# Cross-attention on one core: moving the tiles that TensorE reads to other addresses in SBUF

## The chip, the core and the metric

The kernel runs on one core of a Trainium2 chip. The metric is the device time of one execution in microseconds, as the median of several runs. The engines are TensorE (PE, with its weight loads as PEld), VectorE (DVE), ScalarE (ACT), GpSimd (POOL) and SyncE (SP, which only issues transfers here).

## What is computed

Eight sequences, each with 256 query rows of width 256 and 256 context rows of width 192; 16 heads of 64:

```
h    = layernorm(x) * gamma + beta
Q, K, V = h @ Wq, context @ Wk, context @ Wv      # 16 heads of 64
attn = softmax(Q K^T, axis=-1) * 64 ** -0.5
out  = x + (attn @ V).reshape(...) @ Wo + bo
```

## The kernel before

All weights stay in SBUF, each as a high part (`w_hi`, type float32r) and the rest (`w_lo`); the products of float32r tiles are made in three passes (high by high, high by low, low by high). One step `u` does two of the eight head pairs of a sequence, so four heads, and there are 32 steps, four for each sequence. PE's program in one step, in this order (lines of the profile in brackets):

- `values_rest` (L893): the last pass of V for this step, in two halves of 64 rows, with `c_rest` and `c_t` stationary;
- `scores` (L700): Q stationary, K moving, 12 pairs of 64-row matmuls of 256 columns, the two of a pair side by side in the two halves of the array; Q and K are slots 1 and 0 of `qk_hi` and `qk_lo`;
- `keys_rest` (L771): one pair of 64-row matmuls, `w_lo` stationary;
- `mix` (L729): 16 float32 matmuls, `v_sb` stationary (64 columns), `prob_t` moving;
- `keys` and `queries` (L753, L793): for each of two head pairs 4 and 6 matmuls of 256 columns, weights stationary, the context `c_t` or `h_hi`/`h_lo` moving: 20 in all;
- `output` (L818): 12 matmuls, `mix_hi`/`mix_lo` stationary, weights moving;
- `turn` (L846): 16 float32 transposes of 128 columns, of `prob` against the unit matrix `ident`; once per sequence 4 more each for the context (L675) and x (L683);
- `values` (L880): 8 matmuls, `c_t` stationary, weights moving.

In words of the hardware's program each matmul is a weight load (the stationary operand) and a matmul that streams the moving operand; PE loads the next matmul's weights while the present one streams.

The other engines work beside this. ACT makes the exponentials (L407), the high parts of Q and K (L417), of the mix (L435), V's copy (L395) and half of the copies of the turned probabilities (L460). DVE makes the row maxima (L565), reciprocals, the low parts (L578, L613) and the other copies (L644). POOL scales the probabilities (L319). PE waits at fixed places on them: `scores` on Q's and K's low parts and on the copies of the turned probabilities, `keys_rest` on V's copy, `output` on the mix's low part, `turn` on POOL's scaled probabilities, one wait for each of four heads.

**Homes.** The tensors lie in SBUF in the order in which they are declared, each on the same bytes of every partition; each size is rounded up to a multiple of 32 bytes, and `w_raw`, the first, begins at a multiple of 128 bytes. Worked out from the declared shapes, the homes modulo 128 before the change are:

| tiles | bytes modulo 128 before | after |
|---|---|---|
| `w_raw`, `w_hi`, `w_lo`, `ident`, `v_sb` | 0 | 0 |
| `h_hi`, `h_lo`, `c_t`, `c_rest` | 0 | 64 |
| Q in `qk_hi`, `qk_lo` | 0 | 0 |
| K in `qk_hi`, `qk_lo` | 0 | 64 |
| `x_norm` | 0 | 64 |
| `c_in`, `prob`, `prob_t`, `mix_hi`, `mix_lo` | 96 | 64 |
| `x_in`, `y_sb` | 96 | 0 |

All slices that PE takes of these tiles begin at a multiple of 512 bytes from the tile's (or Q's or K's) beginning, so the table holds for every operand.

Of the kernel before, what the change touches and what calls it, by code (L numbers as in the profile page):

```python
# [5 lines left out]
def cross_attention_block(nc, x, ctx_in, w_q, w_k, w_v, w_o, b_o, gamma, beta, out):  # L6
# [4 lines left out]
    fp32 = mybir.dt.float32  # L11
# [48 lines left out]
    LO_VECTOR = (0, 4, 5, 8, 9, 13, 16)  # L60
    LO_POOL = (1, 2, 3, 6, 7, 10, 11, 12, 14, 15, 17, 18, 19, 20, 21, 22, 23)
    WARM = 6
    V_HALF = GROUP * P // 2

    with ExitStack() as ctx:
# [6 lines left out]
        def sem(name):  # L72
            return ctx.enter_context(nc.semaphore(name))

        w_raw = sb("w_raw", [P, TILES, INNER])
        w_hi = sb("w_hi", [P, TILES, INNER], fp32r)
        w_lo = sb("w_lo", [P, TILES, INNER], fp32r)
        ident = sb("ident", [P, P])
        gamma_c = sb("gamma_c", [P, DT])
        beta_c = sb("beta_c", [P, DT])  # L80
        bo_b = sb("bo_b", [P, D])
        neg_half = sb("neg_half", [P, RT])
        x_in = sb("x_in", [P, 2, RT, D])
        c_in = sb("c_in", [P, 2, RT, D_CTX])
        bn = sb("bn", [P, RT, 6])
        mean_var = sb("mean_var", [P, RT, 2])
        var_eps = sb("var_eps", [P, RT])
        rstd = sb("rstd", [P, RT])
        x_norm = sb("x_norm", [P, RT, D])
        x_bias = sb("x_bias", [P, 2, RT, D])  # L90
        h_full = sb("h_full", [P, DT, ROWS])
        h_hi = sb("h_hi", [P, 2, DT, ROWS], fp32r)
        h_lo = sb("h_lo", [P, 2, DT, ROWS], fp32r)
        c_t = sb("c_t", [P, 2, CT, ROWS], fp32r)
        c_rest = sb("c_rest", [HALF, 2, ROWS], fp32r)
        qk_hi = sb("qk_hi", [P, BATCH, 2, ROWS], fp32r)
        qk_lo = sb("qk_lo", [P, BATCH, 2, ROWS], fp32r)
        v_sb = sb("v_sb", [P, 2, RT, GROUP * P])
        neg_max = sb("neg_max", [P, HEADS, RT])
        sums = sb("sums", [P, HEADS, RT])  # L100
        inv = sb("inv", [P, HEADS, RT])
        prob = sb("prob", [P, HEADS, RT, ROWS])
        prob_t = sb("prob_t", [P, HEADS, RT, ROWS])
        mix_hi = sb("mix_hi", [P, BATCH, ROWS], fp32r)
        mix_lo = sb("mix_lo", [P, BATCH, ROWS], fp32r)
        y_sb = sb("y_sb", [P, 2, RT, D])

        st_ps = [bank(f"st{e}_ps") for e in range(HEADS)]
        mix_ps = bank("mix_ps")
# [237 lines left out]
        def _(act):  # L347
# [38 lines left out]
            def step(u, turns):  # L386
                def values_out(n, ps):
                    act.wait_ge(v_made, n + 1)
                    nc.scalar.activation(v_sb[:, n // RT % 2, n % RT, :], ps[:, :], ACT.Copy)\
                        .then_inc(v_ready, 1)  # L390

                if 2 <= u < STEPS:
                    act.wait_ge(v_made, u + 1 + turns(8))
                    for k, ps in enumerate((w0_ps, w1_ps)):
                        last = nc.scalar.activation(  # L395
                            v_sb[:, u // RT % 2, u % RT, k * V_HALF:(k + 1) * V_HALF],
                            ps[:, 0:V_HALF], ACT.Copy)
                    last.then_inc(v_ready, 1)
                if u == 1:
                    act.wait_ge(c_turned, 2)  # L400
                    context_hi(1, context_bank(1))

                def probabilities(e):
                    if 0 <= u < STEPS:
                        act.wait_ge(max_ready, HEADS * u + e + 1 + turns(32))
                        for r in range(RT):
                            last = nc.scalar.activation(prob[:, e, r, :],  # L407
                                                        st_ps[e][:, r * ROWS:(r + 1) * ROWS],
                                                        ACT.Exp, bias=neg_max[:, e, r:r + 1],
                                                        accum_out=sums[:, e, r:r + 1])  # L410
                        last.then_inc(prob_ready, 1)

                def keys_hi(a):
                    t = BATCH * u + BATCH + a
                    if t < BATCH * STEPS:
                        act.wait_ge(projected, t + 1 + turns(16))
                        nc.scalar.activation(qk_hi[:, a, :, :].rearrange("p a b -> p (a b)"),  # L417
                                             qk_banks(u)[a][:, :], ACT.Copy)\
                            .then_inc(qk_hi_ready, 1)

                if u == 1:
                    weight_hi(14)
                probabilities(0)
                probabilities(1)
                if u in (1, 2):
                    weight_hi({1: 15, 2: 21}[u])
                if u == STEPS:

                    for a in range(BATCH):
                        act.wait_ge(mixed, u + a)  # L430
                        nc.scalar.activation(mix_hi[:, a, :], (mix_ps, w0_ps)[a][:, 0:ROWS],
                                             ACT.Copy).then_inc(mix_hi_ready, 1)
                elif 1 <= u < STEPS:
                    act.wait_ge(mixed, u + turns(8))
                    nc.scalar.activation(mix_hi[:, :, :].rearrange("p a b -> p (a b)"),  # L435
                                         mix_ps[:, :], ACT.Copy).then_inc(mix_hi_ready, 1)
                probabilities(2)
                keys_hi(0)
                if u == -1:
                    weight_hi(6)  # L440
                    weight_hi(7)
                probabilities(3)
                keys_hi(1)
                if u == -1:
                    weight_hi(8)
                    weight_hi(9)
                if u == 0:
                    values_out(0, w0_ps)
                    weight_hi(10)
                    weight_hi(11)  # L450
                    values_out(1, w1_ps)
                if u == 1:
                    weight_hi(16)
                if 0 <= u < STEPS:
                    if u >= 1:

                        act.wait_ge(mixed, u + turns(8))
                    for e in range(0, HEADS, 2):
                        act.wait_ge(turned, HEADS * u + e + 1 + turns(32))
                        nc.scalar.activation(prob_t[:, e, :, :].rearrange("p a b -> p (a b)"),  # L460
                                             st_ps[e][:, :], ACT.Copy)\
                            .then_inc(prob_t_ready[0], 1)
                        if u == 0 and e == 0:
                            weight_hi(12)
                            weight_hi(13)
                b = of_seq(u, TURN_C, 2)
                if b is not None:
                    act.wait_ge(c_turned, b + 1 + turns(2))
                    context_hi(b, context_bank(b))
                b = of_seq(u, TURN_X, 1)  # L470
                if b is not None:

                    act.wait_ge(h_lo_ready, DT * b + turns(4))
                    act.wait_ge(x_turned, b + 1 + turns(2))
                    hidden(b, mix_ps)
                for n in {1: (17, 18, 19, 20), 2: (22, 23)}.get(u, ()):
                    weight_hi(n)
# [7 lines left out]
        def _(dve):  # L485
# [59 lines left out]
            def step(u, turns):  # L545
# [28 lines left out]
                def keys_lo(a):  # L574
                    t = BATCH * u + BATCH + a
                    if t < BATCH * STEPS:
                        dve.wait_ge(qk_hi_ready, t + 1 + turns(16))
                        nc.vector.tensor_tensor(qk_lo[:, a, :, :].rearrange("p a b -> p (a b)"),  # L578
                                                qk_banks(u)[a][:, :],
                                                qk_hi[:, a, :, :].rearrange("p a b -> p (a b)")  # L580
                                                .bitcast(fp32), ALU.subtract)\
                            .then_inc(qk_lo_ready, 1)

                maximum(0)
# [76 lines left out]
        def _(pe):  # L661
# [26 lines left out]
            def scores(u):  # L688
                for a in range(BATCH):
# [6 lines left out]
                    for r in range(RT):  # L696
                        for n, (q, key) in enumerate(passes):
                            for h in range(2):
                                own = slice(h * HALF, (h + 1) * HALF)
                                last = nc.tensor.matmul(  # L700
                                    st_ps[2 * a + h][:, r * ROWS:(r + 1) * ROWS],
                                    q[own, a, 1, r * P:(r + 1) * P], key[own, a, 0, :],
                                    start=n == 0, stop=n == len(passes) - 1)
                                if r == RT - 1 and n == len(passes) - 1:
                                    last.then_inc(scores_made, 1)
# [273 lines left out]
```

## Time and profile before

| | |
|---|---|
| median of 3 runs | 359.43 us (359.4 to 359.51) |
| the profiled execution's own time | 359.32 us |
| its span, first to last instruction | 357.5 us |
| busy: PE, PEld, ACT, DVE, POOL | 97%, 87%, 72%, 68%, 46% |
| TensorE's granted clock | 1.0 throughout (2.4 GHz) |

The profiled execution is 0.11 us under the median, and 1.8 us of it lie outside the span. Matmuls overlap in their records: one takes some 270 to 290 ns from its start to its end, while the next begins 109 to 120 ns after it. So the spacing of the starts tells the rate, and the duration tells a stall of the stream on top of a fixed latency.

### The profile page before, as it was taken

The numbers are of one execution on the slowest core, as the hardware profiler recorded it, in microseconds if no ns is written. First come the engines' busy times: TensorE is split into PE (matmuls) and PEld (weight loads), VectorE is DVE, ScalarE is ACT, GpSimd is POOL, SyncE is SP. The second block draws the span as 40 slices with busy tenths as digits, with TensorE's granted clock in tenths as the row PEclk, the third lists the DMA queues.
The fourth block names the chain that finished last, engine by engine and source line by source line (L and its number), as shares of the span: only waits on it lengthen the run. The fifth ranks groups of instructions, "written<-read, shape, count | busy, mean of one in ns | idle before, by whom it ended". The sixth has DMA issues, their size and how long they took to land.

```text
span 357.5 us, 9031 instructions
## 1 busy us (share of the span) xinstructions
PE 347.6 (97%) x3266; PEld 309.9 (87%) x3266; DVE 244.0 (68%) x534; ACT 256.6 (72%) x800; POOL 164.6 (46%) x321
## 2 busy tenths in 40 slices
PE   5999999999999999999999999999999999999986
PEld 5779888889888889988889988889988889988875
DVE  5897657865768667676677676776576856566654
ACT  4898877776778766878667776777677876677762
POOL 4576894226443263443632465322744325344331
PEclk9999999999999999999999999999999999999999
DMA  6940010020001100020000200002000000000000
GB/s 186 273 131 3 1 53 2 3 81 2 3 0 44 42 2 0 2 81 2 3 2 0 83 2 0 2 2 81 2 2 0 31 2 2 0 4 30 2 2 29
DMA packets 10756, 10.61 MB, mean 30 GB/s; under 512 B 960, under 2 KB 10176, under 8 KB 10720
## 3 DMA queue, kind: packets, MB, share of 16 engines
q1 hardware_dynamic: 10192, 9.64, 8.8%
q8 instruction: 26, 0.43, 0.5%
q10 hardware_dynamic: 416, 0.33, 0.3%
q0 software_dynamic: 112, 0.13, 0.2%
q14 instruction: 10, 0.08, 0.1%
HBM read 8.00 MB, written 2.10 MB: 28 GB/s over the span
## 4 chain that ended last, share of the span: by engine, by line
PE 92%; ACT 3%; DVE 2%; POOL 1%; issue 1%; DVEq 0%; POOLq 0%; ACTq 0%
PE mix_ps L729 16%; PE st_ps L846 15%; PE o_ps L818 12%; PE w_ps L793 12%; PE st_ps L700 12%; PE w_ps L753 10%; PE w_ps L880 8%; PE w_ps L893 3%; ACT prob L407 2%; PE w_ps L771 1%; PE mix_ps L683 1%; PE o_ps L670 1%; PE mix_ps L675 1%; ACT qk_hi L417 0%; DVE w_lo L492 0%
## 5 line engine op out<-in xcount | busy, mean ns | idle before, releaser
L319 POOL TENSOR_SCALAR prob<-prob,inv 128x256 f32<-128x256 f32 x256 | 120.3, 486 | 152.9 <-DVE inv L572 152.9
L407 ACT ACTIVATE prob<-st_ps,neg_max 128x256 f32<-128x256 f32 x256 | 118.4, 476 | 23.6 <-DVE neg_max L565 23.6
L565 DVE TENSOR_REDUCE neg_max<-st_ps 128x2 f32<-128x512 f32 x128 | 82.0, 683 | 27.0 <-PE st_ps L700 25.9
L460 ACT ACTIVATE prob_t<-st_ps 128x512 f32<-128x512 f32 x64 | 38.4, 600 | 40.2 <-PE st_ps L846 40.2
L644 DVE COPY prob_t<-st_ps 128x512 f32<-128x512 f32 x64 | 44.1, 691 | 28.5 <-PE st_ps L846 25.1
L729 PE MATMUL mix_ps<-prob_t,v_sb 128*64 128x256 f32 x504 | 61.4, 386 | 0.1
L846 PE MATMUL st_ps<-ident,prob 128*128 128x128 f32 x512 | 61.1, 273 | 0.0
L846 PEld LDWEIGHTS st_ps<-ident,prob 128*128 128x128 f32 x512 | 56.7, 141 | 0.1
L578 DVE TENSOR_TENSOR qk_lo<-w_ps,qk_hi 128x512 fp32r<-128x512 f32 x62 | 42.8, 690 | 17.7 <-ACT qk_hi L417 17.7
L407 ACT ACTIVATION_READ_ACCUMULATOR prob<-st_ps,neg_max 128x1 f32 x256 | 53.4, 209 | 0.0
L729 PEld LDWEIGHTS mix_ps<-prob_t,v_sb 128*64 128x64 f32 x504 | 33.4, 136 | 17.9 <-issue 0.3
L417 ACT ACTIVATE qk_hi<-w_ps 128x512 fp32r<-128x512 f32 x62 | 37.9, 612 | 1.2 <-PE w_ps L793 1.2
L700 PE MATMUL st_ps<-qk_hi 64*128 64x256 f32 x256 | 36.6, 282 | 0.9 <-DVE prob_t L644 0.6
L753 PEld LDWEIGHTS w_ps<-c_t,w_hi 128*128 128x128 f32 x186 | 26.3, 190 | 11.8 <-issue 11.2
L700 PE MATMUL st_ps<-qk_lo,qk_hi 64*128 64x256 f32 x256 | 36.2, 279 | 0.0
L818 PE MATMUL o_ps<-w_hi,mix_hi 128*128 128x256 f32 x124 | 34.8, 281 | 1.4 <-DVE mix_lo L613 1.4
L700 PE MATMUL st_ps<-qk_hi,qk_lo 64*128 64x256 f32 x256 | 36.1, 279 | 0.0
L753 PE MATMUL w_ps<-c_t,w_hi 128*128 128x256 f32 x186 | 35.5, 300 | 0.0
L818 PE MATMUL o_ps<-w_hi,mix_lo 128*128 128x256 f32 x124 | 34.8, 280 | 0.0
L818 PE MATMUL o_ps<-w_lo,mix_hi 128*128 128x256 f32 x124 | 34.7, 280 | 0.0
L395 ACT ACTIVATE v_sb<-w_ps 128x256 f32<-128x256 f32 x60 | 19.7, 381 | 19.6 <-PE w_ps L893 18.9
L880 PE MATMUL w_ps<-w_hi,c_t 128*128 128x256 f32 x180 | 32.3, 296 | 0.0
(137 smaller groups left out, 646.9 us busy)
## 6 DMA issues: line engine op xcount, KB each, us to landing
x_in<-in_x_dram SPq DMA_DIRECT2D x8, 256.0 KB, 3.2
out_dram<-y_sb SPq DMA_DIRECT2D x7, 256.0 KB, 2.2
c_in<-in_ctx_dram SPq DMA_DIRECT2D x7, 192.0 KB, 3.1
w_raw<-in_L_xattn_Wq_dram SPq DMA_DIRECT2D x8, 128.0 KB, 3.1
w_raw<-in_L_xattn_Wo_dram SPq DMA_DIRECT2D x4, 256.0 KB, 4.4
w_raw<-in_L_xattn_Wk_dram SPq DMA_DIRECT2D x4, 128.0 KB, 4.1
w_raw<-in_L_xattn_Wk_dram SPq DMA_DIRECT2D x8, 64.0 KB, 3.5
w_raw<-in_L_xattn_Wv_dram SPq DMA_DIRECT2D x2, 256.0 KB, 4.7
```

Of the source, the lines that this page charges most:

```text
L319: last = nc.gpsimd.tensor_scalar(prob[:, e, r, :], prob[:, e, r, :], inv[:, e, r:r + 1], SCALE, ALU.mult, ALU.mult)
L407: last = nc.scalar.activation(prob[:, e, r, :], st_ps[e][:, r * ROWS:(r + 1) * ROWS], ACT.Exp, bias=neg_max[:, e, r:r + 1], accum_out=sums ...
L565: nc.vector.tensor_reduce(neg_max[:, e, :], st_ps[e][:, :].rearrange("p (r j) -> p r j", r=RT), AX, ALU.max, negate=True).then_inc(max_rea ...
L578: nc.vector.tensor_tensor(qk_lo[:, a, :, :].rearrange("p a b -> p (a b)"), qk_banks(u)[a][:, :], qk_hi[:, a, :, :].rearrange("p a b -> p ( ...
L644: nc.vector.tensor_copy(prob_t[:, e, :, :].rearrange("p a b -> p (a b)"), st_ps[e][:, :]).then_inc(prob_t_ready[1], 1)
L700: last = nc.tensor.matmul(st_ps[2 * a + h][:, r * ROWS:(r + 1) * ROWS], q[own, a, 1, r * P:(r + 1) * P], key[own, a, 0, :], start=n == 0, ...
L729: last = nc.tensor.matmul(ps[h * HALF:(h + 1) * HALF, first:first + ROWS], v_sb[:, w // RT % 2, j, p * P + h * HALF:p * P + (h + 1) * HALF ...
L753: nc.tensor.matmul(ps[:, 0:ROWS], w[:, i, cols], c_t[:, b % 2, k, :], start=not shared and w is w_hi and i == K0 and k == 0, stop=w is pas ...
L793: last = nc.tensor.matmul(ps[:, ROWS:2 * ROWS], w[:, Q0 + d, cols], h[:, b % 2, d, :], start=n == 0 and d == 0, stop=n == 2 and d == DT - ...
L818: last = nc.tensor.matmul(o_ps[:, r * D:(r + 1) * D], m[:, a, r * P:(r + 1) * P], wt[:, O0 + o, cols], start=s == 0 and a == 0 and n == 0 ...
L846: last = nc.tensor.transpose(st_ps[e][:, j * ROWS + r * P:j * ROWS + (r + 1) * P], prob[:, e, r, j * P:(j + 1) * P], ident[:, :])
L880: nc.tensor.matmul((w0_ps, w1_ps)[a][:, 0:V_HALF], c_t[:, b % 2, k, rows], w[:, i, first:first + V_HALF], start=m == 0, stop=False, skip_g ...
```

## The change

The order of the declarations changes, two unused tiles of 64 bytes (`shift0`, `shift1`) are put in, and the tiles for Q and K get 16 unused elements (64 bytes) behind each slot, which puts K at 64 and Q at 0 modulo 128. The two instructions that write these tiles now write two runs of 256 elements in place of one run of 512, and `scores` takes the first 256 elements of K's slot. No instruction is added, removed or moved.

```
+    SHIFT = 16
...
         ident = sb("ident", [P, P])
+        sb("shift0", [P, SHIFT])
+        h_hi = sb("h_hi", [P, 2, DT, ROWS], fp32r)
+        h_lo = sb("h_lo", [P, 2, DT, ROWS], fp32r)
+        c_t = sb("c_t", [P, 2, CT, ROWS], fp32r)
+        c_rest = sb("c_rest", [HALF, 2, ROWS], fp32r)
+        mix_hi = sb("mix_hi", [P, BATCH, ROWS], fp32r)
+        mix_lo = sb("mix_lo", [P, BATCH, ROWS], fp32r)
+        qk_hi = sb("qk_hi", [P, BATCH, 2, ROWS + SHIFT], fp32r)
+        qk_lo = sb("qk_lo", [P, BATCH, 2, ROWS + SHIFT], fp32r)
+        c_in = sb("c_in", [P, 2, RT, D_CTX])
+        x_norm = sb("x_norm", [P, RT, D])
+        prob = sb("prob", [P, HEADS, RT, ROWS])
+        prob_t = sb("prob_t", [P, HEADS, RT, ROWS])
+        sb("shift1", [P, SHIFT])
+        v_sb = sb("v_sb", [P, 2, RT, GROUP * P])
...
-                        nc.scalar.activation(qk_hi[:, a, :, :].rearrange("p a b -> p (a b)"),
-                                             qk_banks(u)[a][:, :], ACT.Copy)\
+                        nc.scalar.activation(qk_hi[:, a, :, 0:ROWS],
+                                             qk_banks(u)[a][:, :].rearrange("p (a b) -> p a b", b=ROWS),
+                                             ACT.Copy)\
...
-                        nc.vector.tensor_tensor(qk_lo[:, a, :, :].rearrange("p a b -> p (a b)"),
-                                                qk_banks(u)[a][:, :],
-                                                qk_hi[:, a, :, :].rearrange("p a b -> p (a b)")
-                                                .bitcast(fp32), ALU.subtract)\
+                        nc.vector.tensor_tensor(qk_lo[:, a, :, 0:ROWS],
+                                                qk_banks(u)[a][:, :]
+                                                .rearrange("p (a b) -> p a b", b=ROWS),
+                                                qk_hi[:, a, :, 0:ROWS].bitcast(fp32),
+                                                ALU.subtract)\
...
-                                    q[own, a, 1, r * P:(r + 1) * P], key[own, a, 0, :],
+                                    q[own, a, 1, r * P:(r + 1) * P], key[own, a, 0, 0:ROWS],
```

## Rows read from the trace of the kernel before

**Rows 1.** The page: busy time, granted clock by slice, chain that ended last.

```profile
PE 347.6 (97%) x3266; PEld 309.9 (87%) x3266; DVE 244.0 (68%) x534; ACT 256.6 (72%) x800; POOL 164.6 (46%) x321
...
PEclk9999999999999999999999999999999999999999
...
PE 92%; ACT 3%; DVE 2%; POOL 1%; issue 1%; DVEq 0%; POOLq 0%; ACTq 0%
```

**Rows 2.** The waits: who waited for whom: us in total, times, longest.

```profile
PE o_ps L818 <- DVE mix_lo L613: 1.4, 1, 1.4
...
PE st_ps L700 <- DVE prob_t L644: 0.6, 1, 0.6
```

**Rows 3.** Timeline of PE in one step: start us, length us, group and its count.

```profile
151.49 0.28 PE L700 MATMUL st_ps<-qk_hi 64*128 64x256 f32 x2
...
152.93 0.28 PE L771 MATMUL w_ps<-c_rest,w_lo 64*128 64x256 f32 x1
...
155.59 0.40 PE L793 MATMUL w_ps<-h_hi,w_hi 128*128 128x256 f32 x2
...
157.51 0.28 PE L818 MATMUL o_ps<-w_hi,mix_hi 128*128 128x256 f32 x1
...
158.92 1.91 PE L846 MATMUL st_ps<-ident,prob 128*128 128x128 f32 x16
160.67 0.60 PE L683 MATMUL mix_ps<-ident,x_norm 128*128 128x128 f32 x4
...
161.58 0.52 PE L880 MATMUL w_ps<-w_hi,c_t 128*128 128x256 f32 x3
161.94 0.28 PE L880 MATMUL w_ps<-w_lo,c_t 128*128 128x256 f32 x1
```

**Rows 4.** Single lines, whole span: duration ns min/median/max, first and last start.

```profile
L793 PEld LDWEIGHTS w_ps<-h_hi,w_hi x124: 187/192/193, 9.6 to 337.4; 128*128 128x128 f32 x124
L793 PE MATMUL w_ps<-h_hi,w_hi x124: 281/283/301, 9.7 to 337.5; 128*128 128x256 f32 x124
...
L818 PEld LDWEIGHTS o_ps<-w_hi,mix_hi x124: 187/188/193, 28.8 to 348.4; 128*128 128x128 f32 x124
L818 PE MATMUL o_ps<-w_hi,mix_hi x124: 277/280/387, 29.0 to 348.5; 128*128 128x256 f32 x124
...
L700 PE MATMUL st_ps<-qk_lo,qk_hi x256: 274/280/285, 12.9 to 343.7; 64*128 64x256 f32 x128
...
L846 PE MATMUL st_ps<-ident,prob x512: 270/273/273, 19.7 to 350.5; 128*128 128x128 f32 x171
...
L893 PEld LDWEIGHTS w_ps<-w_lo,c_rest x30: 182/183/183, 33.6 to 342.3; 64*128 64x128 f32 x30
...
L867 PE MATMUL w_ps<-w_lo,c_t x4: 392/394/501, 18.0 to 19.5; 128*128 128x512 f32 x4
```

**Rows 5.** Timeline of the weight loads after a pause of the stream.

```profile
151.27 0.18 PEld L893 LDWEIGHTS w_ps<-w_lo,c_t 64*128 64x128 f32 x1
151.37 0.19 PEld L700 LDWEIGHTS st_ps<-qk_hi 64*128 64x128 f32 x2
```

**Rows 6.** Timelines of the same step: what PE waits for, and its loads.

```profile
151.69 0.66 ACT L395 ACTIVATE v_sb<-w_ps 128x256 f32<-128x256 f32 x2
...
152.81 0.19 PEld L771 LDWEIGHTS w_ps<-c_rest,w_lo 64*128 64x128 f32 x1
...
156.07 0.68 DVE L613 TENSOR_TENSOR mix_lo<-mix_ps,mix_hi 128x512 fp32r<-128x512 f32 x1
...
157.40 0.19 PEld L818 LDWEIGHTS o_ps<-w_hi,mix_hi 128*128 128x128 f32 x1
...
158.32 0.93 POOL L319 TENSOR_SCALAR prob<-prob,inv 128x256 f32<-128x256 f32 x2 [0.47 <-DVE inv L572]
```

**Rows 7.** Groups by line: DVE reading 512 elements as 2 x 256 and flat.

```profile
L565 DVE TENSOR_REDUCE neg_max<-st_ps 128x2 f32<-128x512 f32 x128 | 82.0, 683 | 27.0 <-PE st_ps L700 25.9
L644 DVE COPY prob_t<-st_ps 128x512 f32<-128x512 f32 x64 | 44.1, 691 | 28.5 <-PE st_ps L846 25.1
```

More of the change, by code:

```diff
@@ L78, in cross_attention_block @@
         ident = sb("ident", [P, P])
+        sb("shift0", [P, SHIFT])
[13 more added lines that the diff above has]
+        v_sb = sb("v_sb", [P, 2, RT, GROUP * P])
+        x_in = sb("x_in", [P, 2, RT, D])
+        x_bias = sb("x_bias", [P, 2, RT, D])
+        h_full = sb("h_full", [P, DT, ROWS])
+        y_sb = sb("y_sb", [P, 2, RT, D])
+        bo_b = sb("bo_b", [P, D])
         gamma_c = sb("gamma_c", [P, DT])
         beta_c = sb("beta_c", [P, DT])
-        bo_b = sb("bo_b", [P, D])
         neg_half = sb("neg_half", [P, RT])
-        x_in = sb("x_in", [P, 2, RT, D])
-        c_in = sb("c_in", [P, 2, RT, D_CTX])
         bn = sb("bn", [P, RT, 6])
@@ L88, in cross_attention_block @@
         rstd = sb("rstd", [P, RT])
[L89 to L98, printed above, removed]
         neg_max = sb("neg_max", [P, HEADS, RT])
@@ L101, in cross_attention_block @@
         inv = sb("inv", [P, HEADS, RT])
[L102 to L106, printed above, removed]
         st_ps = [bank(f"st{e}_ps") for e in range(HEADS)]
```

## The prediction

> **What bounds the kernel now.** I read the page first: PE is busy 97% of the span and carries 92% of the chain that ended last, at full clock in every slice [rows 1]. The reader should see that nothing but PE's own stream can give more than a few us. The table of waits came next: the largest waits of PE in the steady part are single ones, 1.4 and 0.6 us [rows 2], so PE isn't held up by others. What is left is the rate at which PE's instructions follow each other, so I read the timeline of one step for the spacing of starts, and then the durations by line.
>
> The spacing falls into three classes [rows 3]. Between 155.59 and 157.51 there are 16 matmuls of keys and queries: 1.92 / 16 = 120 ns each. Twelve score pairs from 151.49 to 152.93: 1.44 / 12 = 120 ns a pair. Values, 161.58 to 161.94: 0.36 / 3 = 120. The 12 of the output, 157.51 to 158.92: 1.41 / 12 = 117.5. The 16 transposes, 158.92 to 160.67: 1.75 / 16 = 109.4. Set beside the homes, the first class has both operands at 0 modulo 128 (distance 0), the output has 96 against 0 (32 bytes apart around the circle of 128), and the transposes are plain float32, not float32r, at 96 against 0 or (L683) 0 against 0.
>
> The durations say that the extra time is a stall and not a fixed cost [rows 4]. A transpose takes 273 ns, a query matmul 283, an output matmul 280: 10 and 7 ns more, near the 10.6 and 8.1 ns that the spacings differ by. The best score matmul takes 274, so a float32r stream of 256 columns can go without a stall. Weight loads show the same: 183 ns where no stream runs beside them (L893), 188 beside the output's, 192 beside the queries'. Stream and load slow each other, and by a little less at distance 32 than at distance 0.
>
> **The change, part by part.** Nothing is added or removed, so the sum is a count of spacings times a difference. After the change every pair of a load and a stream is 64 bytes apart modulo 128.
>
> Count. A step has 12 score pairs, 1 pair of L771, 20 keys and queries and 8 values at distance 0, that is 41, of which 2 or 3 begin a group after a change of kind and are spaced by that. I take 39 in 31 steps, 1200, and 12 x 31 = 372 of the output at distance 32.
>
> The price after the change isn't in the trace: no pair stands 64 bytes apart. Its bounds:
> - Best case: no stall, the transposes' 109.4, say 109. Saved 1200 x 11 + 372 x 8.5 ns = 13.2 + 3.2 = 16.4 us.
> - From distance 0 to 32 the spacing fell from 120 to 117.5. Twice as far on the same line gives 115: 1200 x 5 + 372 x 2.5 = 6.0 + 0.9 = 6.9 us.
> - No better than what 32 bytes gave (117.5): 1200 x 2.5 = 3.0 us.
> - Worst that the rows support: distance 64 is like 0 again; then the output goes back to 120, 372 x 2.5 = 0.9 us lost.
>
> I take the middle between the unstalled 109 and 117.5, rounded to 113, because 64 is the farthest that two homes can be from each other on a circle of 128, and because even within the stalled classes single matmuls reach 274 ns [rows 4]. 1200 x 7 + 372 x 4.5 = 8.4 + 1.7 = 10.1 us.
>
> The Trainium skill (TensorE: Matmul & The Clock Gate, Back-to-back issue gap) has a gap of N / 2.4 + 2.5 ns, which is 109 for 256 columns. [...] By that rule as the state after the change the sum would be the best case above, 343.0 us.
>
> Float32 work. The mix (L729) and the transposes change from distance 32 to 64, L683 from 0 to 64. The four transposes of x, at distance 0, last 0.60 us together, which less the last one's 273 ns is 0.327 / 3 = 109 ns a start [rows 3, 4], as those of the probabilities at distance 32. So the distance doesn't seem to matter to float32, and I cost it at nothing. If they began to stall like the others, 24 x 31 x 10 ns = 7.4 us would be lost.
>
> Evacuations. L417 and L578 now write two runs of 256. DVE already reads 512 elements as 2 x 256 in 683 ns and flat in 691 [rows 7], so I take nothing. Should each take 50 ns longer, it lies beside PE's output and transposes and is hidden: `qk` is wanted only in the next step.
>
> **Does the saving reach the end?** A step becomes at most 16.4 / 31 = 0.53 us shorter, and the waits' reserves must cover it [rows 6, 3]. V's copy ends 151.69 + 0.66 = 152.35, the load that waits for it starts at 152.81: reserve 0.46, against at most 12 x 11 = 0.13 saved between. The mix's low part ends 156.75, wanted at 157.40: 0.65, against 20 x 11 = 0.22. POOL ends the fourth head's scaling at 159.25; its transposes are the last four of the sixteen and begin 158.92 + 12 x 0.109 = 160.23: 0.98, against (33 x 11 + 12 x 8.5) = 0.47. All reserves stay, so what PE saves arrives at the end. The few single waits [rows 2] give back none of what is saved before them; I put 0.1 us for that.
>
> Sum against the profiled execution: 359.3 - 10.1 + 0.1 = 349.3, and the median of before is 0.1 above that execution, so 349.4.
>
> **The rivals.**
> - *The stall vanishes altogether* (about 109 to 110): 343.0 us. For it: a float32r matmul at 274 ns exists, and loads of 183. Against: no whole group of float32r matmuls in the rows reaches it. Chance 0.20.
> - *Small*: any distance that isn't 0 gives the output's rate, 117.5: 359.4 - 3.0 = 356.4. For it: the only row with another distance. Chance 0.14.
> - *No effect*: addresses don't enter, and 120 or 117.5 is what a load and its stream cost in float32r, for example because a load of 128 columns bounds the spacing. Time 359.4. Against it: two loads begin 0.10 us apart after a pause of the stream [rows 5], so a load alone doesn't need 120; and at 512 columns, with one load in over 200 ns, a matmul takes 394 ns, where the 273 and the 107 ns of 256 more columns at 2.4 GHz make 380 [rows 4]: 14 ns of stall that no load rate explains. For it: the output and the queries differ in more than their homes (which operand is the weight). Chance 0.14. The Trainium skill (SBUF — State Buffer, Who interferes with whom) gives PE two read ports, one for the moving operand and one for the load, and says that PE never waits on anyone; by it nothing would change, 359.4. The stalled loads and streams above speak against reading it as free of any conflict inside the memory.
> - *Slower*: what conflicts repeats every 64 bytes (or the stream, which runs through addresses twice as fast as the load, meets it half a period later just as often), so distance 64 is as bad as 0, while the output, which now has a better one, loses it: 372 x 2.5 = 0.9 us, 360.3 us. It decides as soon as 1200 spacings gain less than 0.8 ns each. A stall of the float32 part would add to it. Chance 0.14.
> - The forecast, between 110.5 and 116 ns, 345 to 354 us: 0.38.
>
> **How the numbers follow.** Within 0.2% (0.7 us) a measurement of this kernel can't tell a change from none. Faster: 0.38 + 0.20 + 0.14 = 0.72; same 0.14; slower 0.14. Likeliest 349.4. The range must take in the vanished stall at 343.0 and the case of no effect at 359.4, since no effect and slower together are 0.28: 342.6 to 359.8, which leaves out the slower case. The forecast's own range is 345 to 354.
>
> **What would show it in the profile after.** Query and key matmuls at 276 to 279 ns in place of 283, their loads at 184 to 188 in place of 192, the same for scores, values and output; spacing of the 16 matmuls of keys and queries 1.8 us in place of 1.92; transposes still at 109.4 and 273; PE's waits as short as before; L417 and L578 unchanged. It is wrong if durations at L793 stay at 283 (no effect, or period of 64), or if the durations fall and new waits of PE on POOL or DVE appear in each step.

## The result, and the profile after

The changed kernel takes 356.3 us (median of 4 runs, 356.24 to 356.34) against 359.41 for the kernel before beside it: ratio 0.9913, 95% interval 0.9902 to 0.9925. It is 3.1 us or 0.87% faster, where 10.1 us were forecast. The direction was right and the size was not: what was measured is the rival called "small" (356.4).

The page of the changed kernel, its busy times, granted clock and chain:

```profile
span 354.5 us, 9031 instructions
...
PE 344.2 (97%) x3266; PEld 307.0 (87%) x3266; DVE 244.4 (69%) x534; ACT 256.8 (72%) x800; POOL 165.6 (47%) x321
...
PEclk9999999999999999999999999999999999999999
...
PE 91%; ACT 4%; DVE 2%; POOL 1%; issue 1%; DVEq 0%; POOLq 0%; ACTq 0%
```

PE still bounds the kernel, at full clock. Its busy time fell by 3.4 us [rows 1] and the span by 3.0; those of ACT, DVE and POOL rose by 0.2, 0.4 and 1.0 us. The waits are those of before [rows 2]:

```profile
PE o_ps L826 <- DVE mix_lo L621: 1.4, 1, 1.4
PE st_ps L708 <- DVE prob_t L652: 0.6, 1, 0.6
```

So no new wait appeared, and the saving that PE made arrived at the end. The question is only why PE saved so little. Single lines of the changed kernel (duration ns min/median/max), which answer to [rows 4]; L801 is the queries (L793 before), L826 the output (L818), L708 the scores (L700), L854 the transposes (L846):

```profile
L801 PEld LDWEIGHTS w_ps<-h_hi,w_hi x124: 187/188/193, 9.6 to 334.4; 128*128 128x128 f32 x124
L801 PE MATMUL w_ps<-h_hi,w_hi x124: 276/279/303, 9.7 to 334.5; 128*128 128x256 f32 x124
...
L826 PEld LDWEIGHTS o_ps<-w_hi,mix_hi x124: 186/192/192, 28.8 to 345.4; 128*128 128x128 f32 x124
L826 PE MATMUL o_ps<-w_hi,mix_hi x124: 276/281/388, 29.0 to 345.6; 128*128 128x256 f32 x124
...
L708 PE MATMUL st_ps<-qk_lo,qk_hi x256: 272/277/279, 12.9 to 340.7; 64*128 64x256 f32 x128
...
L854 PE MATMUL st_ps<-ident,prob x512: 272/272/273, 19.7 to 347.5; 128*128 128x128 f32 x171
```

The queries' matmuls fell from 283 to 279 ns and their loads from 192 to 188, the scores' from 280 to 277, as the prediction said they would. The output went the other way, which it did not foresee: its matmuls from 280 to 281 ns, its loads from 188 to 192. And the median hides that the lines are of two kinds. The timeline of PE in two steps that follow each other (start us, length us, count) shows them:

```profile
154.44 0.40 PE L801 MATMUL w_ps<-h_hi,w_hi 128*128 128x256 f32 x2
...
156.32 0.29 PE L826 MATMUL o_ps<-w_hi,mix_hi 128*128 128x256 f32 x1
...
156.68 0.28 PE L826 MATMUL o_ps<-w_hi,mix_hi 128*128 128x256 f32 x1
...
157.70 1.91 PE L854 MATMUL st_ps<-ident,prob 128*128 128x128 f32 x16
159.44 0.60 PE L691 MATMUL mix_ps<-ident,x_norm 128*128 128x128 f32 x4
...
165.19 0.39 PE L801 MATMUL w_ps<-h_hi,w_hi 128*128 128x256 f32 x2
...
167.00 0.28 PE L826 MATMUL o_ps<-w_hi,mix_hi 128*128 128x256 f32 x1
...
168.42 1.91 PE L854 MATMUL st_ps<-ident,prob 128*128 128x128 f32 x16
```

First step: 16 matmuls of keys and queries in 156.32 - 154.44 = 1.88 us, 117.5 ns each, and the last nine of the output in 157.70 - 156.68 = 1.02, 113.3 each. Next step: the 16 in 167.00 - 165.19 = 1.81, 113.1 each, and the 12 of the output from 167.00 to the transposes' start at 168.42, 118. The same instructions with the same operands run at one rate or the other for a whole group. Over all 31 steps the last six spacings of a group come to 117.7 or 117.8 ns, or to 113.3, and to nothing between: the queries have 113.3 in 6 steps, the output in 8, never both in one step. I call these the two rhythms. The transposes have 1.74 / 16 = 109 ns, as before.

Summed by function over the whole trace, each spacing counted for the matmul at its end, the spacings of PE's starts went: scores 50.75 to 50.00 us, queries 46.75 to 45.62, values 31.04 to 30.72, output 45.52 to 45.24, keys 40.36 to 40.27, the transposes of x 4.07 to 3.74, all 350.68 to 347.67. Keys and transposes of x belong together: in the start-up PE began the first transposes of x 0.2 us earlier and waited the longer for its first keys, 611 ns in place of 280, so these began at 8.3 us in both. Without that wait the keys of the steady part gained 0.42 us and the transposes of x nothing.

The two instructions that write Q and K, by line (us busy, mean ns of one | idle before):

```profile
L423 ACT ACTIVATE qk_hi<-w_ps 128x512 fp32r<-128x512 f32 x62 | 38.3, 618 | 1.2 <-PE w_ps L801 1.2
...
L585 DVE TENSOR_TENSOR qk_lo<-w_ps,qk_hi 128x512 fp32r<-128x512 f32 x62 | 42.8, 690 | 17.5 <-ACT qk_hi L423 17.5
```

As in the prediction, writing two runs of 256 costs next to nothing (618 and 690 ns, against 612 and 690 before).

### The profile page after: what moved, and what is told of

Same layout as the page of the kernel before. It is cut to its first block, busy times and chain, and to the rows that moved or that the text cites. A ratio compares the mean times of both kernels' runs of the same rounds, so it can differ in the third digit from the quotient of the medians.

```text
span 354.5 us, 9031 instructions
## 1 busy us (share of the span) xinstructions
PE 344.2 (97%) x3266; PEld 307.0 (87%) x3266; DVE 244.4 (69%) x534; ACT 256.8 (72%) x800; POOL 165.6 (47%) x321
## 4 chain that ended last, share of the span: by engine, by line
PE 91%; ACT 4%; DVE 2%; POOL 1%; issue 1%; DVEq 0%; POOLq 0%; ACTq 0%
PE mix_ps L737 16%; PE st_ps L854 15%; PE o_ps L826 12%; PE w_ps L801 12%; PE st_ps L708 12%; PE w_ps L761 10%; PE w_ps L888 8%; PE w_ps L901 3%; ACT prob L413 2%; PE w_ps L779 1%; PE mix_ps L691 1%; PE mix_ps L683 1%; ACT qk_hi L423 0%; DVE w_lo L499 0%; ACT w_hi L359 0%
## 5 line engine op out<-in xcount | busy, mean ns | idle before, releaser
L854 PE MATMUL st_ps<-ident,prob 128*128 128x128 f32 x512 | 61.1, 272 | 0.0
L854 PEld LDWEIGHTS st_ps<-ident,prob 128*128 128x128 f32 x512 | 56.7, 141 | 0.1
L413 ACT ACTIVATION_READ_ACCUMULATOR prob<-st_ps,neg_max 128x1 f32 x256 | 54.2, 212 | 0.0
L708 PE MATMUL st_ps<-qk_hi 64*128 64x256 f32 x256 | 36.4, 280 | 0.9 <-DVE prob_t L652 0.6
L826 PE MATMUL o_ps<-w_hi,mix_hi 128*128 128x256 f32 x124 | 34.8, 281 | 1.4 <-DVE mix_lo L621 1.4
L708 PE MATMUL st_ps<-qk_lo,qk_hi 64*128 64x256 f32 x256 | 36.0, 277 | 0.0
L708 PE MATMUL st_ps<-qk_hi,qk_lo 64*128 64x256 f32 x256 | 35.9, 276 | 0.0
L826 PE MATMUL o_ps<-w_lo,mix_hi 128*128 128x256 f32 x124 | 34.7, 280 | 0.0
L826 PE MATMUL o_ps<-w_hi,mix_lo 128*128 128x256 f32 x124 | 34.7, 280 | 0.0
L579 DVE RECIPROCAL inv<-sums 128x2 f32<-128x2 f32 x128 | 21.0, 164 | 16.7 <-ACT prob L413 13.2
```

The costliest lines, as they stand in the source:

```text
L413: last = nc.scalar.activation(prob[:, e, r, :], st_ps[e][:, r * ROWS:(r + 1) * ROWS], ACT.Exp, bias=neg_max[:, e, r:r + 1], accum_out=sums ...
L708: last = nc.tensor.matmul(st_ps[2 * a + h][:, r * ROWS:(r + 1) * ROWS], q[own, a, 1, r * P:(r + 1) * P], key[own, a, 0, 0:ROWS], start=n = ...
L826: last = nc.tensor.matmul(o_ps[:, r * D:(r + 1) * D], m[:, a, r * P:(r + 1) * P], wt[:, O0 + o, cols], start=s == 0 and a == 0 and n == 0 ...
L854: last = nc.tensor.transpose(st_ps[e][:, j * ROWS + r * P:j * ROWS + (r + 1) * P], prob[:, e, r, j * P:(j + 1) * P], ident[:, :])
```

## The experiments

"Home" is where a tile begins, "distance" is the home of the operand that streams less that of the operand that is loaded as weights. Before each of the kernels below that keeps the reference's work, the kernel before was timed on the same chip (359.34 to 359.40 us).

**One part, none, and other distances.** Experiment 1 keeps every home of before modulo 128 and moves only Q and K apart, experiment 2 moves all homes together, 3 and 4 use 32 and 96 bytes in place of 64, with the helper of experiment 1.

```
# 1: homes as before, by a helper that gives a tile 128 bytes more and begins inside it
+        mix_hi = at("mix_hi", [P, BATCH, ROWS], 96, fp32r)
+        qk_hi = at("qk_hi", [P, BATCH, 2, ROWS + SHIFT], 0, fp32r)
# 2
+        sb("lead", [P, 16])
         w_raw = sb("w_raw", [P, TILES, INNER])
# 3, 4: the changed kernel with 32 or 96 where it has 64, each tile by the helper
-    SHIFT = 16
+    SHIFT = 8        # 4: 24
...
+        h_hi = at("h_hi", [P, 2, DT, ROWS], 32, fp32r)        # 4: 96, and so on
```

> Homes as before the change, only K and Q 64 bytes apart (Q behind 16 unused elements). The distance theory: each load and stream has its own spacing by the distance of its two operands, so only the scores move, 384 pairs from 120 ns to the 117.5 or so that they have in the changed kernel: about 0.8 us, 358.6 us; keys, queries, values stay at 120, the output at 117.5. The rival, that the gain comes from the tiles' new order as a whole or from other engines' tiles, expects 359.4 here.

> The kernel before with one unused tile of 64 bytes ahead of all others: every home moves by 64 bytes, every distance stays. The distance theory: 359.4 us, queries at exactly 120 ns again. The rival, that it is the absolute home of the moving or stationary tile that counts (64 instead of 0), expects some of the 3.1 us, 356.3 to 358.5.

> As the changed kernel, with 32 bytes in place of 64 for every shifted tile and for Q behind K. Theory A, only distance 0 is bad and all others are alike: 356.3 us. Theory B, the stall falls with the distance up to 64: between, about 357.9. Theory C, a stream and its loads lock into one of a few fixed rhythms, and which ones exist depends on the distance: groups at one constant spacing each, not 120, some other mix than the changed kernel's 113.3 and 117.8; no direction given.

> As the changed kernel, with 96 bytes in place of 64. Theory A: 356.3 us. Theory B, counted around a circle of 128: as at 32 bytes, about 357.9, with the signs of the distances exchanged (what is the stationary tile 32 ahead there is 32 behind here). Theory C: constant spacings, not necessarily those of 32 bytes.

| | us | ratio to before, 95% |
|---|---|---|
| 1 Q and K alone | 358.58 | 0.9979 (0.997 to 0.9989) |
| 2 all moved by 64 | 359.34 | 0.9999 (0.999 to 1.0009) |
| 3 distance 32 modulo 128 | 357.92 | 0.9961 (0.9946 to 0.9975) |
| 4 distance 96 modulo 128 | 359.33 | 0.9999 (0.9989 to 1.0008) |

Experiment 2 shows that moving every home by 64 bytes with all distances kept changes nothing. Experiments 3 and 4 refute a circle of 128 that is the same both ways round, on which "64 is the farthest" rested: 32 and 96 would be alike, and are 1.4 us apart. Experiment 1 met its number, 358.6, by chance: the scores' sum fell by only 0.40 us (50.75 to 50.35), while the queries, whose homes modulo 128 were those of before, fell by 0.59 (46.75 to 46.16), the keys rose by 0.24 and the output by 0.22. Its padding moved tiles by odd multiples of 128, the low parts of h and of the mix among them. So something beyond the address modulo 128 counts. Experiments 3 and 4 have the same padding, so in them too the low parts of h and of the mix stand 128 bytes off the distance in the table.

**A table of distances.** Experiment 5 leaves out the kernel's work. PE alone runs groups of 24 loads and matmuls, float32r, 256 columns, the weights at home 0, and the moving operand's home in steps of 4 bytes.

```
+            for k in range(24):
+                nc.tensor.matmul(ps[:, 0:256], wide[:, (k % 8) * P:(k % 8) * P + P],
+                                 mv[i][:, home // 4:home // 4 + 256], start=True, stop=True)
```

> A table of the disputed price: PE alone runs 24 pairs of a weight load (128 columns, float32r) and a matmul of 256 columns, waits for their end, and goes on to the next run. The weights lie at 0 modulo 128, the moving tile at 0, 4, 8, ... 124; then 128 to 2048 bytes more at 0 and 64; the weights' slice not walked; 1 to 8 float32 matmuls ahead of a run; and 512 columns. The kernel leaves out all of the reference's work and copies x to the output. Theory B (the stall falls with the distance on a circle of 128): spacing 120 ns at 0, falling to 113 at 64, the same at 32 and 96. Theory C (fixed rhythms): each home has one constant spacing from a few values (120, 117.8, 113.3), 64 has 113.3 or 117.8 by how its run begins, that is by the number of matmuls ahead; 32 and 96 differ from each other, since the stream moves twice as fast as the load. Modulo 128 is the whole rule if 128 to 2048 bytes more change nothing; if they do, higher bits of the address count.

Timeline of PE: mv_aa has home 0, mv_ab 4, mv_ac 8, mv_ad 12, mv_ba 64, mv_bm 112. The last two rows are a further pass, with homes 128 and 192. A row's length holds 23 spacings, of which the first after the group's entry is longer.

```profile
52.54 3.11 PE L62 MATMUL ps<-mv_aa,wide 128*128 128x256 f32 x24
55.70 3.20 PE L62 MATMUL ps<-mv_ab,wide 128*128 128x256 f32 x24
58.97 3.26 PE L62 MATMUL ps<-mv_ac,wide 128*128 128x256 f32 x24
62.28 3.07 PE L62 MATMUL ps<-mv_ad,wide 128*128 128x256 f32 x24
...
103.53 3.09 PE L62 MATMUL ps<-mv_ba,wide 128*128 128x256 f32 x24
...
141.82 3.02 PE L62 MATMUL ps<-mv_bm,wide 128*128 128x256 f32 x24
...
256.46 3.12 PE L62 MATMUL ps<-mv_aa,wide 128*128 128x256 f32 x24
259.63 3.01 PE L62 MATMUL ps<-mv_ba,wide 128*128 128x256 f32 x24
```

The last twelve spacings of a group, in ns, by distance: 0: 120.0, 4: 123.3, 8: 126.7, 12: 116.7, 28: 115.6, 32: 116.7, 64: 117.75, 96: 120.0, 112: 113.3, 116: 121.7. The second pass gave the same to 0.1 ns. Homes 256, 512, 1024 and 2048 bytes further on give what 0 and 64 give, but 128 further does not: 118.8 in place of 120.0, 113.3 in place of 117.75. So at home 0 the period is 256 (at 64 and 192 the rate can differ at one and the same home, see experiment 8), and the function is ragged. Three findings speak of the price: at distance 64 it is 117.75, in both passes and again after each of 1 to 8 float32 matmuls ahead; the forecast's 113 is met at 112 and 192 only, and no home of the 32 is below 113.3. A moving operand of 512 columns takes 227 ns at distance 0, 233 at 32, 229 at 64.

**Parts of the change.** Experiment 6 is the changed kernel with Q where K is (distance 0 for the scores alone). Experiment 7 has the change's order of declarations and no shift, so that all operands, the output's too, stand at distance 0 modulo 128.

```
# 6
-        qk_hi = sb("qk_hi", [P, BATCH, 2, ROWS + SHIFT], fp32r)
+        qk_hi = sb("qk_hi", [P, BATCH, 2, ROWS], fp32r)
# 7: as 6, and
-        sb("shift0", [P, SHIFT])
-        sb("shift1", [P, SHIFT])
```

> The changed kernel with no unused elements behind K and Q: both at 64, distance 0, all else as changed. Sum of parts: the changed kernel's 356.3 plus the 0.8 us that the scores alone gave: 357.1 us, scores at 120 ns a pair again. The rival, that a group's rhythm depends on the group before it, lets other groups change as well: more than 0.3 us off 357.1.

> The new order of the tiles, without the 64-byte tiles and without the elements behind K and Q: every tile that PE reads is at 0. Modulo 128 is the whole rule: keys, queries, values, scores at 120 ns as before, the output from 117.5 to 120, 372 x 2.5 = 0.9 us: 360.3 us. The rival, that higher address bits count (the tiles stand elsewhere beyond modulo 128): queries not at a constant 120.

Experiment 7: 360.24 us, 1.0026 (1.0016 to 1.0035), expected 360.3. In 368 of its 372 output spacings it has 120 ns, so the output's 117.5 before did come from its distance. Experiment 6: 356.21 us, 0.9913 (0.9896 to 0.9929), where adding up parts asks for 357.1. The scores gave back half of what they had won (50.00 to 50.38 us, where 50.75 stood before), but lines that were not touched changed: every output group has 113.3 now, and no group of queries has.

```profile
L826 PEld LDWEIGHTS o_ps<-w_hi,mix_hi x124: 187/188/188, 28.8 to 345.3; 128*128 128x128 f32 x124
L826 PE MATMUL o_ps<-w_hi,mix_hi x124: 276/276/386, 28.9 to 345.4; 128*128 128x256 f32 x124
```

That is the output's line in experiment 6: median 276 ns, against 281 in the changed kernel. Nothing declared ahead of `qk_hi` moved, so the operands of the queries and of the output lie on the very bytes that they have in the changed kernel. The price of a pair of operands is therefore not a function of their distance alone, nor of their full addresses, and parts don't add up.

**What chooses the rhythm.** Experiment 8, again without the kernel's work, has the homes from 128 to 252, and then the same group at distance 192 after a growing number of float32 matmuls, and right behind another group.

```
+            for before in range(1, 9):
+                warm(before)                  # float32, 128 columns
+                done(run(24, 192))            # 24 pairs at distance 192
+            for first, then in ((192, 64), (64, 192), (0, 64), (0, 192)):
+                run(first // 8, first)
+                done(run(then // 8, then))
```

> The table of run e5 goes on: the moving tile's home from 128 to 252 bytes beyond the weights' (counted modulo 256), then the 64-row pairs at distances 0 to 240 in steps of 16, the weights moved instead of the moving tile, 1 to 8 float32 matmuls ahead of a run at 192, and runs that follow a run at another distance without a pause. It leaves out all of the reference's work. In e5 the moving tile at 192 ran at 113.3 ns and at 64 at 117.8, and 128 bytes more at 0 weren't the same as 0, while 256 more were: if the rule has a period of 256, 192 gives 113.3 whatever comes ahead, and this half of the table differs from the first half; if the period is 128 and 113.3 was luck of the entry, this half repeats the first and 192 gives 117.8 after some of the preambles.

Timeline of PE: mv_bi at home 192 after 1 to 5 float32 matmuls (L79 counts each of them twice):

```profile
213.69 3.07 PE L62 MATMUL ps<-mv_bi,wide 128*128 128x256 f32 x24
216.82 0.71 PE L79 MATMUL qs<-plain 128*128 128x128 f32 x4
217.29 2.99 PE L62 MATMUL ps<-mv_bi,wide 128*128 128x256 f32 x24
220.34 0.94 PE L79 MATMUL qs<-plain 128*128 128x128 f32 x6
221.03 2.98 PE L62 MATMUL ps<-mv_bi,wide 128*128 128x256 f32 x24
224.07 1.16 PE L79 MATMUL qs<-plain 128*128 128x128 f32 x8
224.98 3.07 PE L62 MATMUL ps<-mv_bi,wide 128*128 128x256 f32 x24
228.11 1.38 PE L79 MATMUL qs<-plain 128*128 128x128 f32 x10
229.25 2.98 PE L62 MATMUL ps<-mv_bi,wide 128*128 128x256 f32 x24
```

One group, two lengths: 3.07 us is a steady 117.8 ns, 2.98 a steady 113.3. After 1 to 8 float32 matmuls it has 117.8, 113.3, 113.3, 117.8, 113.3, 117.8, 113.3, 117.8. So both rhythms exist at one distance, and a group keeps the one it has fallen into. Nothing but the entry differs between the eight groups, which points to the entry as what decides; each number of float32 matmuls was run once. Without a pause between, 192 behind 0 runs at 113.3, 64 behind 0 at 117.8, and both 192 behind 64 and 64 behind 192 at 117.8. Of the homes from 128 to 252, 136 has 120.0 where 8 had 126.7, and 240 has 117.3 where 112 had 113.3, so the table does not repeat after 128; 192 has 117.8 in this pass and had 113.3 in experiment 5. With the moving operand left at home 0 and the weights moved by 64, 128 and 192 instead, the groups have 113.3, 118.3 and 117.8, values that distances 192, 128 and 64 have when the moving operand is the one that moves: a second sign that the distance counts and not the home. At distance 0 experiment 5 found 120.0 after every number of float32 matmuls, as the queries of the kernel before have it: that distance has neither rhythm. With half the rows, as in the scores, pairs take 120 ns at distance 0, 117.8 at 32, and 113.3 at 64, 112 and 192.

**Only one distance, and same homes.** Experiment 9 puts every moving operand 192 bytes beyond its weights modulo 256. Experiment 10 keeps that and gives the output's two operands the homes that the queries' have, and to the slots of the two head pairs in Q's and K's tiles the same homes modulo 256. 11 does the same at distance 64.

```
# 9, homes modulo 256: W_k, W_q 128; W_v, W_o 0; context, h, mix 64; K 64, Q 128
+        h_hi = at("h_hi", [P, 2, DT, ROWS], 64, fp32r)
# 10
-        mix_hi = at("mix_hi", [P, BATCH, ROWS], 64, fp32r)
+        mix_hi = at("mix_hi", [P, BATCH, ROWS], 128, fp32r)    # and W_o at 64
+        qk_hi = at("qk_hi", [P, BATCH, 2 * (ROWS + SHIFT) + 32], 64, fp32r)
# 11: context, h, K, W_o 192; W_k, W_q, mix, Q 128; W_v 0
+        h_hi = at("h_hi", [P, 2, DT, ROWS], 192, fp32r)
+        mix_hi = at("mix_hi", [P, BATCH, ROWS], 128, fp32r)
```

> The whole kernel with every moving operand of a float32r matmul 192 bytes beyond its stationary operand modulo 256 (the weights of Q and K at 128, those of V and the output at 0, the context, h and the mix at 64, K 64 and Q 128). If the distance modulo 256 is the rule: all groups at 113.3 ns, 1200 x 6.7 + 372 x 4.2 = 9.6 us saved, about 350 us. If only the distance modulo 128 counts, it is the changed kernel again: 356.3. If 113.3 and 117.8 are two rhythms of the same distance and the entry chooses: between, 352 to 356.

> As e9, but the output's operands get the very homes that keys and queries have (stationary 128, moving 64 modulo 256), so a rhythm can go on from the one group into the other without meeting another distance between; the slots of Q and K repeat every 256-multiple, so both head pairs of the scores have the same homes. If a group inherits its rhythm from the one ahead: the output at 113.3 ns like the queries, 372 x 4.5 = 1.7 us under e9, and the scores near 113.3 a pair, some 1.2 us: about 352.3 us. If the output's 118 in e9 had another cause (its own homes, or the weights on the moving side), it stays: 354 to 355.

> The mirror of e10: the same layout with each moving operand 64 bytes beyond its stationary one modulo 256 (128 and 192) instead of 192. By the tables, 64 falls into the rhythm of 117.8 almost always and 192 about every second time into that of 113.3: keys, queries and output mostly at 117.8, 355.5 to 356.5 us. If distances 64 and 192 are alike and only the carrying over counts: the time of e10, about 352.3.

| | us | ratio to before, 95% | queries at 113.3 | output at 113.3 | equal in a step |
|---|---|---|---|---|---|
| changed kernel | 356.3 | 0.9913 | 6 of 31 | 8 of 31 | 17 |
| 9 distance 192 | 355.08 | 0.9882 (0.9865 to 0.9898) | 30 | 3 | 2 |
| 10 with same homes | 353.71 | 0.9841 (0.9828 to 0.9854) | 30 | 30 | 31 |
| 11 distance 64, same homes | 353.14 | 0.9826 (0.9813 to 0.984) | 31 | 29 | 29 |

What experiment 10 gains on 9 is the output's alone (45.49 to 44.12 us); the scores, for which 1.2 us were expected, went from 50.06 to 50.33. Experiment 11 was expected to be the poorer of the last two if 64 were the poorer distance (355.5 to 356.5), and to take about 352.3 if the two distances were alike. It is the best version measured, 6.3 us under the kernel before and 3.2 under the changed one. Its single lines, queries and output:

```profile
L823 PE MATMUL w_ps<-h_hi,wq_hi x124: 276/276/280, 9.9 to 331.4; 128*128 128x256 f32 x124
...
L848 PE MATMUL o_ps<-wo_hi,mix_hi x124: 276/276/387, 28.9 to 342.4; 128*128 128x256 f32 x124
```

And its timeline, where keys, queries and output run through in one rhythm:

```profile
153.28 0.39 PE L823 MATMUL w_ps<-h_hi,wq_hi 128*128 128x256 f32 x2
...
155.09 0.28 PE L848 MATMUL o_ps<-wo_hi,mix_hi 128*128 128x256 f32 x1
...
156.46 1.91 PE L876 MATMUL st_ps<-ident,prob 128*128 128x128 f32 x16
```

155.09 - 153.28 = 1.81 us for 16, 113.1 each; 156.46 - 155.09 = 1.37 for 12, 114 each with the change of kind at the end.

**The output's homes alone.** In experiment 11 other tiles moved too. Experiment 12 is the changed kernel, in which only the output's operands move, to the queries' homes.

```
-        mix_hi = sb("mix_hi", [P, BATCH, ROWS], fp32r)
+        mix_hi = sb("mix_hi", [P, BATCH * ROWS + 64], fp32r)[:, 48:48 + BATCH * ROWS]
+            rest = sb(name + "_o", [P, 2 * INNER + 64], fp32r)[:, 16:16 + 2 * INNER]    # W_o
```

> The changed kernel with one thing more: the mix moves to 128 and the output's weights to 192 modulo 256, the homes that the stationary and the moving operands of keys and queries have there; all else keeps its home modulo 256. If a group hands its rhythm on when the homes stay, each step's output runs at the spacing of its queries: in the changed kernel 24 of 32 groups of queries at 117.8 and the rest at 113.3, so little gain, 356.0 to 356.3 us, but step by step the two spacings agree, where before they didn't. If the rhythm of the queries changes too, because what comes ahead of them now ends at another moment, the agreement must still hold and the time can fall to 353. If rhythms aren't handed on, output and queries disagree in some steps as in the changed kernel.

It takes 356.33 us, 0.9916 (0.9903 to 0.993). Two steps of its timeline, one of each rhythm:

```profile
154.50 0.39 PE L816 MATMUL w_ps<-h_hi,w_hi 128*128 128x256 f32 x2
...
156.31 0.28 PE L841 MATMUL o_ps<-w_hi_o,mix_hi 128*128 128x256 f32 x1
...
157.67 1.91 PE L869 MATMUL st_ps<-ident,prob 128*128 128x128 f32 x16
...
165.19 0.40 PE L816 MATMUL w_ps<-h_hi,w_hi 128*128 128x256 f32 x2
...
167.07 0.28 PE L841 MATMUL o_ps<-w_hi_o,mix_hi 128*128 128x256 f32 x1
...
168.49 1.91 PE L869 MATMUL st_ps<-ident,prob 128*128 128x128 f32 x16
```

Queries and keys take 1.81 us and then 1.88 for 16, the output 1.36 and then 1.42 for 12. The output has the queries' rhythm in 31 of 31 steps (113.3 in 6 of them), where in the changed kernel it had the other in 14. A group whose operands stand where those of the group ahead stand goes on in its rhythm. The same distance is not enough for that: in experiment 9 queries and output have the same distance at different homes, and agree in 2 of 31 steps. The move gains nothing by itself, because the queries' rhythm is still mostly 117.8.

## Why the prediction was wrong in size and right in sign

- **What bounds the kernel**: right. PE's rate alone; the 3.0 us by which the sum of its spacings fell came off the span, and no reserve of [rows 3, 6] was used up.
- **The stall comes from where load and stream stand**: right. The kernels of this study that do the same work differ in homes and, as the homes of Q and K ask for, in how these are written, and they range from 353.14 to 360.24 us. Experiment 2 speaks for the distance and against the home, experiment 7 shows that the output's 117.5 was a matter of distance too. The Trainium skill (SBUF — State Buffer, Who interferes with whom) gives the load and the stream a port each and says that PE waits on nobody; these runs do not agree with leaving homes out on that ground: with the same instructions of PE, they differ by up to 7.1 us.
- **The price after the change, "I take the middle between the unstalled 109 and 117.5, rounded to 113"**: this step failed. Where it put 7 ns a spacing for keys, queries, scores and values and 4.5 for the output, the queries gained 3.1, the scores 2.0 and the output 0.8. None of its reasons held. "64 is the farthest that two homes can be from each other on a circle of 128" supposed a smooth function with period 128. The table shows a ragged one with period 256, in which 64 costs 117.75, no better than 32 (116.7). And the bound 109 was that of another kind of matmul, float32 transposes of 128 columns: float32r of 256 columns never came under 113.3 in a steady group, in no home of the tables and no kernel. Single durations did not bear on the rate either: the scores' go down to 272 ns in the changed kernel, while nearly all of their groups settle at 117.8. The Trainium skill (TensorE: Matmul & The Clock Gate, Back-to-back issue gap) has 109 for 256 columns, as the gap of an isolated matmul, and these matmuls do not keep it. The transposes are no evidence for it: they stream 128 columns, for which the Trainium skill has 134 cycles in the same place, about 56 ns at 2.4 GHz, and they are 109 ns apart. Even the best version of this study (353.14) is 10.1 us above the rival built on it (343.0).
- **The measured price**: queries at 117.8 in 25 steps and 113.3 in 6, on average (25 x 117.8 + 6 x 113.3) / 31 = 116.9, so 3.1 ns a spacing and, summed, 1.13 us, where 7 ns were taken. Scores 0.75 us over 384 pairs, 2.0 ns each. Output 0.28 us in place of 1.7, or 0.8 ns over 372. Values 0.32 us, where 31 x 8 x 7 ns would be 1.7. Keys 0.42 us with the start-up's wait left out, again where 1.7 was taken. These are 2.9 of the 3.0 us of the span.
- **Counting spacings and multiplying by a price for each distance**: this form of the sum failed too. It missed experiment 6 by 0.9 us, met experiment 1 by chance, and had experiment 11 wrong by over 2 us for the case that 64 is the poorer distance. At distances 64 and 192 a group's rate is one of two, and what runs ahead of it bears on which.
- **Float32 work and evacuations at nothing**: right, spacing 109 and duration 272 ns for the transposes, 618 and 690 for the two writes.
- **Rivals**: "small" had the size (117.5 for everything, 3.0 us), partly by luck: its one rate stood for a mixture of 117.8 and 113.3, in which the output gained too. "The stall vanishes" happened in no kernel and at no home. "No effect" and "slower" fell with the result. The slower one's mechanism, that all at distance 0 costs the output 0.9 us, is what experiment 7 measured at 0.90 us (360.24 - 359.34).

**What stays open.** What in the entry chooses the rhythm isn't known: the queries' operands of experiments 11 and 12 have the same homes, and run at 113.3 in 31 steps in the one and in 6 in the other; what runs ahead of them and the places of the tiles beyond 256 bytes differ. The repeat every four steps in the changed kernel (output at 113.3, queries at 113.3 in the next step) goes unexplained. Distance 64 never gave 113.3 with PE alone (experiments 5 and 8), and gave it in 31 steps of experiment 11. The scores' pairs should reach 113.3 at distances 64 and 192 by experiment 8, and summed to 50.0 to 50.4 us in every kernel that has one of these distances between Q and K. What happens inside the memory is argued from spacings, not seen.

## What to carry to other kernels

Where back-to-back float32r matmuls with a new load each bound a kernel, look at the spacing of the starts in one group. Both operands at the same place modulo 256 gave 120 ns for 256 columns at full clock (so did some other distances, such as 96), and moving tiles to a distance of 64 or 192 bytes is worth 2% (117.8) to 6% (113.3) of those matmuls' time. Don't price a layout from one row or add up parts; time whole layouts, keep one distance for all groups, and give groups that follow each other without a pause the same two homes. And before taking a bound for the price "with no stall" from another kind of matmul, find a whole group of the same kind that reaches it.

## What the runs showed of the hardware that was not expected

- Load and float32r stream slow each other by an amount that changes within 4 bytes (120.0, 123.3, 126.7, 116.7 ns at 0, 4, 8, 12) and does not repeat after 128 bytes (126.7 at 8, 120.0 at 136); at the homes 0 and 64, where it was tried, it does after 256.
- At distances 64 and 192 a group of equal matmuls has a steady rate out of two (113.3 and 117.8 ns) at one and the same layout. It keeps it to the group's end, and hands it to the next group if that has the same homes (91 of 93 steps in experiments 10 to 12, against 2 of 31 in experiment 9).
- No layout took float32r of 256 columns below 113.3 ns, which leaves 4 ns to the 109 of float32 transposes of 128 columns.
